# Coefficients of a Householder step with two row blocks: on TensorE from x itself, in place of a product and sum on VectorE

## The reference

```python
deg = jnp.sum(A, axis=0) + jnp.sum(A, axis=1) - jnp.diagonal(A)
d_inv_sqrt = jnp.where(deg > 0, jax.lax.rsqrt(deg), 0.0)
L_norm = d_inv_sqrt[:, None] * (jnp.diag(deg) - A) * d_inv_sqrt[None, :]
_, U = jnp.linalg.eigh(L_norm)
agg = jnp.einsum('mn,bnd->bmd', U.T, features)
```

## Time and profile before

| | |
|---|---|
| median of three runs | 6107.22 us (6106.77 to 6107.6) |
| the profiled execution | 6111.74 us, its span 6110.0 us |
| PE busy | 3713.2 us (61%), 22240 matmul passes |
| PEld busy | 2438.2 us (40%) |
| DVE busy | 4434.1 us (73%), 25392 instructions |
| ACT busy | 1216.2 us (20%) |
| granted TensorE clock, mean over the span | 0.644 of full speed |
| DMA | 17.05 MB, under 1% of the engines' time in nearly all of the span |

### The profile page before, as it was taken

One profiled execution on the slowest core, in us unless ns is written; L12 is line 12 of the kernel. 1 busy time (PEld: TensorE's weight loads), 2 busy tenths in 40 slices (PEclk: granted clock), 3 DMA queues, 4 the chain that ended last, 5 costly groups with the idle time before them and its releaser, 6 DMA issues. The chain is left out here.

```text
span 6110.0 us, 79662 instructions
## 1 busy us (share of the span) xinstructions
PE 3713.2 (61%) x22240; PEld 2438.2 (40%) x22240; DVE 4434.1 (73%) x25392; ACT 1216.2 (20%) x3608; POOL 16.8 (0%) x30
## 2 busy tenths in 40 slices
PE   4666655555555566633233333397885899986674
PEld 4555554445555555510000000143332655552352
DVE  7888888888888877789999999712225677624457
ACT  1111111111212122222122222214332111100000
POOL 0000000000000000000000000000000000000000
PEclk9755555555555555555555555598897699987876
DMA  1000000000000000000000000000000000000001
GB/s 36 2 2 2 2 1 1 1 1 1 1 1 1 1 1 1 1 0 0 0 0 0 0 0 0 21 1 0 0 0 0 1 0 0 0 0 0 0 0 28
DMA packets 14090, 17.05 MB, mean 3 GB/s; under 512 B 624, under 2 KB 10000, under 8 KB 13712
## 3 DMA queue, kind: packets, MB, share of 16 engines
q1 hardware_dynamic: 10896, 9.44, 0.5%
q10 hardware_dynamic: 2352, 2.69, 0.2%
q0 software_dynamic: 464, 0.55, 0.0%
HBM read 8.47 MB, written 4.19 MB: 2 GB/s over the span
## 5 line engine op out<-in xcount | busy, mean ns | idle before, releaser
L803 DVE SCALAR_TENSOR_TENSOR poly<-poly,off,term 128x60 f32<-128x60 f32 x2560 | 611.4, 275 | 0.0
L795 DVE SCALAR_TENSOR_TENSOR term<-cut,rows,poly 128x60 f32<-128x60 f32 x2560 | 598.8, 276 | 13.7 <-DVE poly L785 4.3
L565 PE MATMUL totals<-pp_sum,ones 128*128 128x2 f32 x768 | 225.5, 363 | 524.5 <-DVE pp_sum L410 524.5
L726 PE MATMUL both_signs<-signs,identb 128*128 128x480 bf16 x320 | 186.2, 582 | 567.7 <-PEq L65 567.7
L1014 PE MATMUL horner_ps<-horner,S 128*128 128x512 f32 x1024 | 460.6, 592 | 0.0
L515 PE MATMUL row_e<-vwv 128*128 128x2 f32 (+30 forms) x988 | 301.7, 396 | 198.9 <-DVE x_parts L424 198.9
L526 PEld LDWEIGHTS product<-x_parts,A_parts 128*128 128x128 bf16 x11136 | 405.3, 111 | 42.9 <-DVE A_parts L340 42.9
L565 PEld LDWEIGHTS totals<-pp_sum,ones 128*128 128x128 f32 x768 | 192.5, 311 | 563.5 <-DVE pp_sum L410 563.5
L526 PE MATMUL product<-x_parts,A_parts 128*128 128x3 bf16 x11136 | 359.9, 167 | 41.9 <-DVE A_parts L340 41.9
L1534 PE MATMUL gate_ps<-h_sb,wih_t 128*128 x504 | 316.2, 788 | 82.2 <-PEq L65 82.2
L515 PEld LDWEIGHTS row_e<-vwv 128*128 128x128 f32 x988 | 258.7, 322 | 213.0 <-issue 213.0
(11 more groups left out here) (485 smaller groups left out, 8182.2 us busy)
## 6 DMA issues: line engine op xcount, KB each, us to landing
out_dram<-x_sb SPq DMA_DIRECT2D x4, 1024.0 KB, 7.3
adj_sb<-adj_dram SPq DMA_DIRECT2D x1, 1024.0 KB, 5.8
alpha<-L_gnn_alpha_train_dram POOLq DMA_DIRECT2D x1, 256.0 KB, 5.5
edge_row<-L_gnn_src_dram POOLq DMA_DIRECT2D x1, 128.0 KB, 5.4
edge_row<-L_gnn_dst_dram POOLq DMA_DIRECT2D x1, 128.0 KB, 5.8
w<-L_gnn_Wg_dram ACTq DMA_DIRECT2D x2, 64.0 KB, 3.9
w<-L_gnn_W_dram ACTq DMA_DIRECT2D x2, 64.0 KB, 3.4
x_sb<-x_dram SPq DMA_DIRECT2D x4, 0.5 KB, 10.4
```

The costliest lines, as they stand in the source:

```text
L565: pe.matmul(totals[:, 0:2], k.ones[:], pp_sum[:], start=True, stop=True).then_inc(dot_ready, 1)
L726: pe.matmul(here, identb[:], rows_of(b, way, 0), start=True, stop=False)
L795: pair(dve.scalar_tensor_tensor(out=term[:, way, :], in0=flat, scalar=rows[:, way, row:row + 1], in1=poly[:, b, way, s + 1, :], op0=ALU.su ...
L803: pair(dve.scalar_tensor_tensor(out=poly[:, b, way, s + 2, :], in0=poly[:, b, way, s, :], scalar=off2[:, way, row:row + 1], in1=term[:, wa ...
```

## The change

Where two row blocks are active, VectorE no longer makes `x_on_pairs` and its sum, and TensorE no longer waits for them. Instead `coefs` issues one fp32 matmul for each block, with the block's column of x broadcast as weights and the block's pairs as moving operand, and the two add up in PSUM (`start` on the first, `stop` on the last). With three or four blocks nothing changes, and with one block the loop gives the single matmul that stood there before.

```diff
@@ step(), end of VectorE's part
-                if n > 1 and not last:
+                if n >= 3 and not last:
                     mark(dve.tensor_tensor(on_pairs[:, c0:C, 0:2 * j + 2].rearrange("p c (j t) -> p c j t", t=2),
                                            vwv[:, c0:C, 2:3 + j, 1:3],
@@ coefs(), TensorE
-                if c0 == C - 1:
-                    pe.matmul(coef[:, 0:2 * j].rearrange("p (j t) -> p j t", t=2), vwv[:, c0, j % 2, 1:2].broadcast_to([P, P]),
-                              vwv[:, c0, 2:2 + j, 1:3], start=True, stop=True).then_inc(coef_ready, 1)
-                else:
+                if C - c0 >= 3:
                     pe.matmul(coef[:, 0:2 * j], k.ones[:], on_pairs_sum[:, 0:2 * j], start=True, stop=True)\
                         .then_inc(coef_ready, 1)
+                    return
+                for c in range(c0, C):
+                    last = pe.matmul(coef[:, 0:2 * j].rearrange("p (j t) -> p j t", t=2), vwv[:, c, j % 2, 1:2].broadcast_to([P, P]),
+                                     vwv[:, c, 2:2 + j, 1:3], start=(c == c0), stop=(c == C - 1))
+                last.then_inc(coef_ready, 1)
@@ the step on TensorE
                     if j and n <= 2:
-                        if n == 2:
-                            pe.wait_ge(dve_did, pos["on_pairs", row])
                         coefs(j, c0)
```

## The result

| | before | changed |
|---|---|---|
| median | 6107.75 us (6106.77 to 6109.35, 7 runs) | 6127.24 us (6126.07 to 6128.08, 7 runs) |
| ratio | | 1.0031, 95% interval 1.002 to 1.0043 |
| profiled execution, its span | 6111.74, 6110.0 | 6127.24, 6125.5 |

The change makes the kernel 19.5 us slower, 0.3%. The forecast was 24 us (6131), the range 6122 to 6139.

A forecast was written before the change was run, and what follows sets the result against it. A loop of hand-overs between VectorE, TensorE and ScalarE was taken to bound the step, coefficients having 0.25 us of slack. Later prod_x adds 6.0 us a panel, 24 for four: 6107.2 + 24 = 6131 us, range 6122 to 6139.

The forecast's parts named there:

- The two VectorE instructions are worth nothing: Two-block steps: removing x_on_pairs and its sum, about 50 us of VectorE busy time, gains nothing; the reciprocal waits for the root.
- TensorE's wait goes for nothing: Ahead of coef: the wait for the sum was over before the products began, so coef starts when it did.
- Two passes more cost 0.42 us: Coefficients' matmul in two-block steps: four fp32 passes instead of two add 0.42 us, taken from the norm's four passes.
- The bounds of 0.08 and 0.52: Limits for the two added passes: 0.08 us from bf16 product spacing, 0.52 if new weights wait for columns.
- The rival of coefficients in time: Between coef's start and prod_x: passes below 0.13 us apart land before VectorE comes, so no change, 6107 us; chance 5 in 100.
- prod_x comes 0.24, 0.21, 0.14 us later: VectorE's prod_x, waiting for coef, starts this much later at j = 1, 11 and 31 (2, 22 and 62 columns).
- The delay reaches the totals whole: VectorE's instructions from prod_x to pp_sum pass the delay on whole to the next x: 6.0 us a panel, 24 for four.
- The other panels keep their code: Outside the two-block panels nothing was added to the sum; with one block the loop gives the same single matmul.
- VectorE's busy time falls by 50 us: A sign of being right: VectorE's busy time falls by about 50 us while the span grows.
- The clock: Rival: TensorE's granted clock, 0.50 in two-block stretches, might rise with its larger share; would not help, time the forecast's.

The follow-up runs named there:

- four passes with and without the pair: With: the changed kernel, but VectorE again makes x_on_pairs and its sum, unread, 6132.8 us. Without: the changed kernel itself, 6127.24 us.
- one matmul: Changed kernel with coefficients made from the last row block alone, the other block's share left out in two-block steps: 6100.9 us.
- two memsets: Kernel with the coefficients ahead, plus two one-element VectorE memsets in each of the 124 two-block steps: 6107.2 us.
- the coefficients ahead: Changed kernel with the four-pass coefficients issued ahead of the products instead of behind them in two-block steps: 6101.2 us.
- the short norm: Kernel with the coefficients ahead, where VectorE makes xx and its sum for two blocks and TensorE's norm takes two passes: 6105.9 us.

## Why the prediction was right, point by point

- *The two VectorE instructions are worth nothing.* Right in the steps: with and without the pair the reciprocal starts 1.70 us after x. The prediction's "worth nothing" was wrong for the kernel: 5.6, 6.4 and 6.0 us in three comparisons (four passes with and without the pair, the kernel before against one matmul, two memsets against none). It did not come from less work, as the memsets show.
- *TensorE's wait goes for nothing.* Right: coef starts 1.97 to 2.05 us after x as before.
- *Two passes more cost 0.42 us.* Right: coef takes 0.99 (forecast 0.98), 1.03 (1.02) and 1.09 (1.09) us at 2, 22 and 62 columns. The bounds of 0.08 and 0.52 weren't needed. The rival of coefficients in time needed passes less than 0.13 us apart; they stand 0.21 apart, and it falls. The Trainium skill's rule for weight loads ("TensorE: Matmul & The Clock Gate", LDWEIGHTS), half of this, does not hold for the fp32 passes of these steps.
- *prod_x comes 0.24, 0.21, 0.14 us later.* Right within 0.02: 3.00, 3.05, 3.18 us after x in place of 2.75, 2.82, 3.03.
- *The delay reaches the totals whole.* It reached them, with something on top: the steps grew by 0.26, 0.24 and 0.16 us. The forecast for j = 11 was 4.91 us, measured 4.94. Over all 124 steps prod_x starts 0.20 us later on the mean, 24.7 us in all where 24 were summed, and the way from its start to the totals is 0.02 us longer, 2.2 us in all, as prod_x itself is once it waits (221 against 201 ns). That term was missing; together the steps grew by 26.9 us.
- *The other panels keep their code.* This is the mis-sized term: "keep their code" was taken for "keep their time". In the tridiagonal stage that holds to 1 us, but the bisection and the tail got 3.5 to 5 and 2.6 to 3 us shorter, since VectorE's list ahead of them is 248 instructions shorter. The two errors have opposite signs: 26.5 - 7 = 19.5. The range doesn't hold by luck: with either error alone the time would have been some 6134 or 6124 us, inside it still.
- *VectorE's busy time falls by 50 us.* 54 in the steps, by the groups of the pair (27.0 and 27.4 us in that stretch before); the page shows 34. Neighbours on VectorE overlap, and the busy time counts an overlap once: 130.9 us a panel before, 122.9 and 122.4 after, 8 us for each of four panels.
- *The clock* stayed at 0.50, as expected.

Between the kernel before and the changed one, the tail's 3 us stand ahead of L1307 (66.3 us against 63.0, and 597.5 against 597.7 behind it), in a stretch where VectorE waits for fp32 matmuls. The first 40 us of the tail, before and changed, with the columns of the earlier trace rows:

```profile
5434.30:5474.30 40.00, 25.10 (x124) 21.70 (x122) 14.14 (x25) 0.59 (x1) 0.29 (x1) 0.66 0.00 0
...
5452.80:5492.80 40.00, 24.97 (x137) 21.86 (x136) 14.16 (x25) 0.58 (x1) 0.29 (x1) 0.79 0.00 0
```

TensorE is busy for as long, and does 137 passes in place of 124, at a mean granted clock of 0.79 in place of 0.66. The clock is 0.66 to 0.70 in the four profiles with a list of 25392 and 0.79 in the six others. At the upper level (1.00, 2.4 GHz) these passes start 0.11 us apart, at the lower (0.50, 1.2 GHz) 0.21 (L1235, from 5442.56 and from 5443.90 us in the kernel before). So the 3 us are time at the lower level.

What stays open: why the clock takes another course there with another list; why the next packet of instructions is not on its way before the loop jumps back to it; and the 0.6 us at L819.

## What to carry to other kernels

In a chain of hand-overs, write down for each result when it lands and when it is taken, from the same event; moving work from a busy engine to an idle one pays only if its result lands before it is taken, and here 0.25 us of slack, less 0.04 for the hand-over, met 0.42 us of added passes. Look for the order first: the same four passes ahead of work that can wait cost nothing. And before a difference of 0.1% is put down to an edit, compare the stages that the edit leaves alone: the fastest version here, with the coefficients ahead (6101.2 us, 6 us below before), owes that lead to the length of its instruction list and not to its arithmetic, since the same kernel with 248 idle memsets takes 6107.2.

## What the runs showed of the hardware

- The time of an unedited VectorE loop depends on how many instructions stand before it: 1271.2 to 1271.8 us in five profiles, 1274.7 to 1276.4 in four, 1279.1 in one; the value goes with the length of the list, not with what it does. Longer is not slower: the short norm's list of 25400 has the value of 25144, 256 or two packets of instructions away, and not of 25392.
- After each jump back VectorE goes on 1.8 to 2.0 us after the start of an 8 KB packet on the instruction queue, and if the end of a packet lies 2 or 6 instructions behind the loop's first, it stands still again for 1.1 to 2.1 us.
- VectorE's reading of fresh coefficients: 221 ns on the mean after a wait, 201 without, same shapes.
- From the end of x or of xx_sum on VectorE to the norm's matmul it took 0.14 to 0.15 us, from the end of pp_sum to the totals' matmul 0.05, from TensorE to VectorE or ScalarE 0.03 to 0.04.
- In the two-block steps, at a granted clock of 0.50, fp32 passes start 0.21 us apart for 2 to 62 columns. In the tail, runs of fp32 passes with 128 columns start 0.21 us apart at 0.50 and 0.11 at 1.00. The 48 bf16 products take 1.42 us at a granted clock of 1.00 as at 0.50.
